# Vision tower, 64 images: the product of dt and x moves from GpSimd to VectorE, the order of work is laid out afresh, and the first loads are split

## What is computed

```python
h = patches(x) @ W.T + b                          # 16x16 patches of 3 colours
xb, z = split(h @ in_proj.T)                      # 512 channels each
xb = silu(causal_conv4(xb))
dt_in, B, C = split(xb @ x_proj.T)                # 1, 16 and 16 numbers a token
dt = softplus(dt_in * dt_w + dt_b)
h_n(t) = exp(dt * A_n) * h_n(t-1) + (xb * dt) * B_n    # 16 states a channel
y = sum_n h_n * C_n + xb * D
h = layernorm(h + (layernorm(y) * silu(z)) @ out_w.T)
h = layernorm(h + gated_ffn(h))                   # mixes each token with the one before it
h = layernorm(h + 8_head_attention(h))
h = layernorm(h + top2_of_8_experts(h))
```

## Time and profile before

| | us |
|---|---|
| median of 3 runs | 4496.96 (4495.98 to 4497.75) |
| span of the profiled execution, first to last instruction | 4498.6 |
| busy TensorE, GpSimd, ScalarE, VectorE | 4150.4, 4031.8, 3836.7, 3749.3 |
| mean granted TensorE clock over the span | 0.979 of full speed |

### The profile page before, as it was taken

The page is one execution under the profiler, slowest core; times in us unless marked ns, Lnnn a source line. Parts: engine busy times, 40 slices in busy tenths (PEclk is TensorE's granted clock), DMA queues, the critical chain, the costliest instruction groups (busy, mean ns, idle before and its releaser), DMA issues.

```text
span 4498.6 us, 92573 instructions
## 1 busy us (share of the span) xinstructions
PE 4150.4 (92%) x32128; PEld 3625.2 (81%) x32128; DVE 3749.3 (83%) x7246; ACT 3836.7 (85%) x10114; POOL 4031.8 (90%) x2120
## 2 busy tenths in 40 slices
PE   4689999999999999999999999999999999999986
PEld 3678888888888888888888888888888888888775
DVE  2678889888888888888988988888888888898853
ACT  3688988988988998898898898898899889889852
POOL 3999999999999999999999999999999999999930
PEclk8799999999999999999999999999999999999987
DMA  4332332233233233233233223323323323323200
GB/s 100 71 71 65 75 82 75 67 82 78 69 78 80 70 77 87 67 76 82 69 73 82 75 67 82 78 70 77 80 69 76 89 66 76 82 68 74 70 19 29
DMA packets 730609, 328.75 MB, mean 73 GB/s; under 512 B 631542, under 2 KB 655392, under 8 KB 729888
## 3 DMA queue, kind: packets, MB, share of 16 engines
q1 hardware_dynamic: 730144, 322.83, 29.1%
HBM read 307.82 MB, written 14.90 MB: 72 GB/s over the span
## 4 chain that ended last, share of the span: by engine, by line
PE 65%; ACT 19%; DVE 5%; POOL 5%; issue 3%; DMA 1%; SPq 1%; DVEq 0%; POOLq 0%; ACTq 0%
PE G L738 15%; PE YB L608 13%; PE G L575 6%; ACT dA L915 5%; PE SB L679 4%; PE G L660 4%; PE SB L584 4%; PE G L628 4%; PE G L652 3%; POOL X L497 2%; ACT pr L987 2%; PE SB L689 2%; POOL X L486 2%; DVE xbs L1110 2%; PE G L636 2%
## 5 line engine op out<-in xcount | busy, mean ns | idle before, releaser
L1145 DVE TENSOR_TENSOR_SCAN X<-dA,X 128x392 f32<-128x392 f32 x2048 | 1870.5, 955 | 142.0 <-ACT dA L915 96.7
L497 POOL TENSOR_TENSOR X<-X,Cb 128x1568 f32<-128x1568 f32 x512 | 1802.8, 3521 | 129.7 <-DVE X L1145 127.2
L486 POOL TENSOR_TENSOR X<-u,Bb 128x1568 f32<-128x1568 f32 x512 | 1804.2, 3524 | 0.1
L915 ACT ACTIVATE dA<-dt,negA 128x195 f32<-128x195 f32 x4096 | 1510.5, 414 | 64.6 <-DVE X L1145 46.0
L608 PE MATMUL YB<-idn,X 128*98 128x128 f32 x8192 | 1086.3, 276 | 23.6 <-POOL X L497 23.6
L608 PEld LDWEIGHTS YB<-idn,X 128*98 128x98 f32 x8192 | 908.2, 129 | 155.8 <-issue 102.1
L738 PE MATMUL G<-hg,we 128*128 128x196 f32 x4096 | 711.2, 332 | 8.3 <-DVE hg L1256 6.1
L738 PEld LDWEIGHTS G<-hg,we 128*128 128x128 f32 x4096 | 684.8, 192 | 10.8 <-issue 7.5
L987 ACT ACTIVATE pr<-pr,nmx 98x196 f32<-98x196 f32 x1024 | 453.4, 446 | 9.1 <-DVE nmx L1192 9.1
L584 PE MATMUL SB<-hT,win 128*128 128x196 f32 x2048 | 368.2, 333 | 14.5 <-ACT pT L998 5.6
L584 PEld LDWEIGHTS SB<-hT,win 128*128 128x128 f32 x2048 | 335.5, 190 | 29.5 <-issue 21.3
(11 more groups left out here) (151 smaller groups left out, 6554.7 us busy)
## 6 DMA issues: line engine op xcount, KB each, us to landing
Bb<-proj_rows SPq DMA_DIRECT2D x256, 392.0 KB, 4.2
Cb<-proj_rows SPq DMA_DIRECT2D x256, 392.0 KB, 3.8
Gb<-gate_rows SPq DMA_DIRECT2D x64, 784.0 KB, 4.1
px<-in_x SPq DMA_DIRECT2D x1024, 36.8 KB
out<-ob SPq DMA_DIRECT2D x64, 196.0 KB
dtin<-proj_rows SPq DMA_DIRECT2D x64, 98.0 KB, 3.0
we<-in_w_e SPq DMA_DIRECT2D x1, 2048.0 KB
proj_rows<-pj SPq DMA_DIRECT2D x64, 25.3 KB
```

The costliest lines, as they stand in the source:

```text
L486: tt(X[(WIDES * s + w) % RING][:], u[q % 2][:, c:c + 1, :].broadcast_to([P, NW, T]), Bb[:, n0:n0 + NW, :], ALU.mult).then_inc(xs_pool, 1)
L497: tt(t[:], t[:], Cb[:, n0:n0 + NW, :], ALU.mult).then_inc(prod_ready, 1)
L915: last = go(dA[i % DRING][:, j, 1:T], dt_[q % 2][:, c, 1:T], ACT.Exp, scale=negA[:, c, n:n + 1])
L1145: v.tensor_tensor_scan(t, dA[i % DRING].rearrange("p n t -> p (n t)"), t, 0.0, ALU.mult, ALU.add).then_inc(scan_done, 1)
```

## The change

1. `make_u` moves from GpSimd to VectorE. It reads dt and xbs, both in SBUF, and writes u. Its slot goes from -14 to -9, and GpSimd's wait for `xs_pool` in it falls away.
2. Nearly every slot constant and the order of the list in every `step` function are new. The work is the same, the six filling products of `keep_busy` among it.
3. The loads are split. ScalarE's queue issues six first (identity, patch weights, convolution and in_proj: `head`); SP issues the first image's pixels and then the other 26 loads. TensorE starts when the six have landed. VectorE scales the two convolution constants first (`conv_ready`), and prepares the other twelve inside `gate_x` of the first image; ScalarE waits for them in `tanh_of_x` of the first image (`late_weights`).

The diff, cut to its core:

```diff
-AT_LOAD = -46
-AT_PATCH = (-30, -28, -26,)
+AT_LOAD = -57
+AT_PATCH = (-30, -28, -27,)
...
-AT_EMBED = -25
+AT_EMBED = -24
...
-AT_U = -14
+AT_U = -9
...
-AT_ATT_STD = 59
-AT_ATT_NORM = 61
+AT_ATT_STD = 62
+AT_ATT_NORM = 66
...
-        loads = [(wtok, w_tok), (btok, b_tok), (win, w_in), (cw, conv_w), (cb, conv_b), (wxp, w_xproj),
+        head = [(idn, ident), (wtok, w_tok), (btok, b_tok), (cw, conv_w), (cb, conv_b), (win, w_in)]
+        loads = [(wxp, w_xproj),
...
-            def make_u(s, q):
-                pool.wait_ge(dt_ready, s + 1)
-                after(pool, xs_pool, WIDES * (s - 1))
-                tt(u[q % 2][:], dt_[q % 2][:], xbs[:], ALU.mult).then_inc(u_ready, 1)
...
+            def make_u(s, q):
+
+                dve.wait_ge(dt_ready, s + 1)
+                v.tensor_tensor(u[q % 2][:], dt_[q % 2][:], xbs[:], ALU.mult).then_inc(u_ready, 1)
...
-            pe.wait_ge(w_landed, W_ALL)
-            pe.wait_ge(const_ready, CONSTS)
+            pe.wait_ge(head_landed, W_HEAD)
...
+                if s == 0:
+                    late_weights()
                 go(S.tile, xbs[:].rearrange("p (a b) t -> p a (b t)", a=2), ACT.Tanh).then_inc(tanh_x, 1)
...
+            def late_weights():
+                act.wait_ge(w_landed, W_ALL)
+                go(negA[:], negA[:], ACT.Exp).then_inc(nega_exp, 1)
+                act.wait_ge(zeros_ready, ZEROS)
+                act.wait_ge(const_ready, CONSTS)
...
+            for dst, src in head:
+                act.dma_start(dst[:], src).then_inc(head_landed, 16)
+            act.wait_ge(head_landed, W_HEAD)
+            act.wait_ge(conv_ready, CONV)
```

More of the change, by code:

```diff
@@ L393, in _, with load_rest @@
         def _(sp):
+            def load_rest():
+                for dst, src in loads:
+                    sp.dma_start(dst[:], src).then_inc(w_landed, 16)
             def load(s):
@@ L437, in at @@
                         return live(b, par, g, slot)
+                    for s, q in at(AT_LOAD):
+                        load(s)
+                        if s == 0:
+                            load_rest()
                     for s, q in at(AT_DT_LOAD):
@@ L459, in step @@
                         spread_gates(s)
[L460 to L464, removed]
+                    for s, q in at(AT_PROJ_STORE):
+                        store_proj(s)
+                    for ng in range(GC):
+                        n0 = NG * ng
+                        for s, q in at(AT_C[ng]):
+                            after(sp, prod_ready, WIDES * s - WC + ng // 2 + 1)
+                            spread_rows(s, Cb[:, n0:n0 + NG, :], 1 + STATES + n0, NG, C_landed[ng])
             schedule(sp, step)
@@ L516, in step @@
                     for k in range(WIDES):
[L517 to L518 removed]
+                        for s, q in at(2 * k + AT_TIMES):
+                            times_c(s, k)
                     for s, q in at(AT_MOE_STD):
@@ L755, in at @@
                         return live(b, par, g, slot)
[L757 to L761, removed]
+                    for s, q in at(AT_V):
+                        pe.wait_ge(ksq_ready, s + 1)
+                        channel_major(s, "v", wv, ka)
+                    for s, q in at(AT_TURN_Y):
+                        turn_y(s)
+                    for s, q in at(AT_GATE):
+                        gate(s, q)
                     for s, q in at(AT_H1T):
@@ L764, in step @@
                         turn(s, "h1T", h1)
[L765 to L799, removed]
+                    for s, q in at(AT_EMBED):
+                        embed(s)
                     for s, q in at(AT_QK):
@@ L815, in step @@
                             scores(s, n)
[L816 to L820, removed]
+                    for s, q in at(AT_MOE_T):
+                        turn_moe(s)
+                    for part in range(3):
+                        for s, q in at(AT_PATCH[part]):
+                            patches(s, part)
+                    for s, q in at(AT_WARM[3]):
+                        keep_busy(WARM[3])
+                    for i in range(BLK):
+                        for s, q in at(AT_TURN_AV[i]):
+                            turn_values(s, i)
                     for s, q in at(AT_OUT):
@@ L1038, in step @@
                         drain_turned(s, "h3T", h3T[q % 2][:], where["h3T"].drained)
+                    for s, q in at(AT_ATT_NORM):
+                        if s > 0:
+                            filled("h3T2", s - 1)
+                        normalise(s, "att", lambda k: att[:, k, :], h3, normed["att"])
+                    for s, q in at(AT_Z_OUT):
+                        tanh_of_z(s)
+                    for part in range(3):
+                        for s, q in at(AT_PATCH_OUT[part]):
+                            drain_patches(s, part)
@@ new lines, in step @@
+                    for s, q in at(AT_KSQ):
+                        act.wait_ge(where["k"].drained, where["k"].count("k", s))
+                        go(ka[:], ka[:], ACT.Square).then_inc(ksq_ready, 1)
+                    for s, q in at(AT_YG):
+                        scale_y(s)
+                    for s, q in at(AT_EMBED_OUT):
+                        drain_embed(s, q)
+                    for s, q in at(AT_SOFT):
+                        softplus(s, q)
+                    for s, q in at(AT_TAP):
+                        first_tap(s)
@@ new lines, in step @@
+                    for s, q in at(AT_H2T_OUT):
+                        drain_turned(s, "h2T", h2T[:], where["h2T"].drained)
+                    for n in range(UNITS):
+                        for s, q in at(AT_PROBS[n]):
+                            probs(s, q, n)
+                    for s, q in at(AT_QK_OUT):
+                        drain_qk(s)
+                    for c in range(IC):
+                        for s, q in at(AT_Y_OUT[c]):
+                            drain_y(s, c)
+                    for s, q in at(AT_XPROJ_OUT):
+                        drain_proj(s)
@@ new lines, in step @@
+                    for s, q in at(AT_XD):
+                        times_d(s, q)
+                    for n in range(UNITS):
+                        for s, q in at(AT_PR[n]):
+                            drain_scores(s, n)
+                    for n in range(UNITS):
+                        for s, q in at(AT_PT[n]):
+                            drain_pT(s, n)
+                    for k in range(GROUPS):
+                        for s, q in at(k + AT_DECAY):
+                            decay(s, q, k)
@@ L1292, in step @@
                             taps(s, which)
+                    for s, q in at(AT_OUT_STATS):
+                        o = filled("outT", s)
+                        moments(s, "out", lambda k: o[0:TB, k * D:(k + 1) * D])
+                    for s, q in at(AT_MIX):
+                        token_mix(s)
+                    for s, q in at(AT_FFN_STATS):
+                        o = filled("ffnT", s)
+                        moments(s, "ffn", lambda k: o[0:TB, k * D:(k + 1) * D])
                     for i in range(BLK):
```

322 lines of the change are left out of this document (151 added, 171 removed).

## The result

The changed kernel takes **4631.27 us** (median; 4628.21 to 4632.74) against 4497.35 before: a ratio of 1.0295, 95% interval [1.028, 1.031]. It is 3% slower. Forecast were 4400 and a range of 4325 to 4500; the time lies outside, on the side of the third rival, which had put it at 4563.

What follows compares the result with a forecast made beforehand. It took a loop over ScalarE (some 15 us) and TensorE (51 us), 66.62 us an image, as the bound. 4498.6 - 82.6 (order) - 14 (start) = 4402.0, less 1.6 for the median: 4400 us; range 4325 to 4500.

Steps and rivals of the forecast that it cites:

- the third rival: u on VectorE and GpSimd's multiplications block each other, beyond 3.13 us it costs: slower, 4563 us; chance 0.14.
- u comes to VectorE: u on VectorE takes 0.97 us, hidden ahead of project_out and paid for before the scans; nothing added on the path.
- The far end: Upper bound for u on VectorE: it waits out a 3.52 us GpSimd multiplication, 4.49 us; GpSimd stands still 0.97.
- the low end: Lower bound for VectorE and GpSimd getting in each other's way over u: nothing, which the forecast took.
- Slots and orders: New slots and list orders on all engines: 1.4 us an image won, 82.6 us over 59 periods; bounds 0 and 156.
- the four covered waits: TensorE's waits at embed, turn_y, hT's transpose and the second patch transpose go, 1.77 us an image together.
- The floor of 63.97 us for TensorE: TensorE's period of 66.62 us less its 2.65 us of waits; with the same work it cannot go lower.
- the first rival: Another loop holds the period, new order opening as many waits as it shuts; only start won: 4483 us; chance 0.17.
- u leaves GpSimd: GpSimd's work falls from 63.0 to 61.15 us an image; alone worth nothing where TensorE holds the chain.
- The start: Split loads let TensorE start 16.5 to 21.2 us sooner; net gain taken as 14 us, bounds 0 and 18.
- A tanh at 30 to 33: Sign of a right forecast at the start: first tanh on ScalarE at 30 to 33 us, before at 48.87.

Runs made afterwards that it cites:

- e2: Changed kernel with u still on VectorE in the same place, but first operand from PSUM, dt left out for all but two images: 4459.48 us, ratio 0.9915.
- e4: Kernel before the change with only the start split (six loads on ScalarE's queue, the rest behind the first pixels): 4485.25 us, ratio 0.997.
- e1: Changed kernel with only u put back on GpSimd at slot -14; new order and split start stay: 4467.05 us, ratio 0.9928.
- e7: Changed kernel with u back on GpSimd and all of ScalarE's copies of y moved ahead of patches and softplus: 4588.35 us, ratio 1.0202.
- e9: Changed kernel with u back on GpSimd and only two of ScalarE's four copies of y moved ahead: 4455.95 us, ratio 0.9914.
- e10: Changed kernel with u on VectorE from PSUM (dt left out) and two copies of y moved ahead: 4453.66 us, median of three, ratio 0.99.
- e8: Changed kernel with u on VectorE from PSUM (dt left out) and all copies of y moved ahead: 4581.38 us, ratio 1.0184.
- e5: Changed kernel with u one place earlier in VectorE's order, between the two pairs of scans: 4499.71 us, ratio 1.0002.
- e6: Changed kernel with u two steps later in VectorE's order, behind the statistics and ahead of the last scans: 4579.77 us, ratio 1.0181.
- e3: Kernel before the change with only u moved to VectorE, ahead of gate_y, both inputs in SBUF; old order and start: 4652.04 us, ratio 1.0343.

## Why the prediction was wrong, point by point

**The step that failed** is in "u comes to VectorE": "I take nothing on the path, since u is one instruction an image." The far end stood beside it, 4.49 us for u and 0.97 for GpSimd. Measured are 3.49 and 0.72. One instruction an image is enough, because what stands behind it had too little slack: y, the scans, the taps and then ScalarE's qm and km follow in one chain. e2 against the changed kernel gives the price, with engine, place, size and count of u equal: periods of 66.32 and 69.05 us, so 59 x 2.73 = 161 of the 172 us. In the fill, where two u took 9.02 and 10.99 us, the chain falls 16 us behind (its first such product starts at 372.92 and not at 356.97). Together that is 5 us more than the 172, which this count does not settle. The choice of the low end went by zs, which has one operand in PSUM; the row was near in size and not in what mattered.

**The third rival** had the right mechanism and too low a price. It let 3.13 of 4.49 us be soaked up, by VectorE's 1.28 us of waiting and GpSimd's saved 1.85. At the measured 3.49 us its rule would have asked 0.36 us an image. Beside e2, next to nothing of u's lengthening was soaked up: u is 2.52 us longer, and the period 2.73. How much of this is GpSimd's 0.72 no run tells apart. GpSimd's saved 1.85 did not pay: its waits for scans grew by more than that, over 2 us an image (38.6 us against 17.6 in the window). So the rival's 4563 was 68 us too low.

The Trainium skill, page "SBUF — State Buffer", section "Who interferes with whom", was named for that rival: issue order decides who blocks, and the other side blocks fully. The traces agree in the steady part: u waits out the multiplication that it meets (3.49, 2.19 and 1.70 us in three places), and the next GpSimd instruction waits out u (4.25 for 3.53, 0.92 for 0.20). The same section says that a VectorE instruction with at most one SBUF input, outside certain modes, does not contend; the 967 ns of e2 agree.

**"Slots and orders", 1.4 us an image**, was mis-sized: e4 against e1 gives (66.61 - 66.33) = 0.28, with 66.61 = (4090.32 - 360.25) / 56 and 66.33 = (4080.86 - 366.14) / 56 from their chains. Each of the four covered waits did go. But adding up waits of TensorE is no sum of time: 1.92 us for ysb came in their place, and the wait for probs grew from 0.88 to 1.35. The nearest case is embed, whose 0.60 for patT the prediction took as covered by the D term and a group of sums. In e1 that D term (L615) itself waits, 0.63 of the 1.92 us, for a ysb that ScalarE copies right behind patT, so ScalarE's list still holds up embed (L585):

```profile
4054.45 0.10 ACT patT L866
...
4054.78 0.37 ACT ysb L942
...
4055.20 0.43 PE YB L615 x2
...
4056.50 3.98 PE G L585 x24
```

The floor of 63.97 us for TensorE did not hold either: in e1 it waits 1.92 + 1.35 = 3.27 of 66.33 us, which leaves 63.06; why the same products took less is not known. All this was the first rival, "a new order can open as many waits as it shuts", whose time of 4483 would have been near without the blocking (4459 to 4467). So even with u harmless the forecast was 60 us too low. e7 and e9 support it: with the waits on ysb taken away in part, others come, and in e9 the chain goes over VectorE's scans and taps, ScalarE's qm and km, TensorE, softplus and back. Which single handover closes that loop was not settled.

**"u leaves GpSimd": nothing** was right within the noise: e10 lies 2 us under e9, e8 7 under e7 and e2 8 under e1, each pair with overlapping intervals.

**"The start", 14 us** was near: 12.8 in e4. Partly that is luck, as its parts were off: the 16 pixel DMAs took 13.0 us to issue, more than the 6.7 to 11.4 assumed, so the first transpose came at 15.52 and not at 10 to 14, and the tanh at 36.63 and not at 30 to 33. TensorE started 15.3 us sooner, and the way from there to the tanh grew from 18.06 to 21.11. A tanh at 30 to 33 would have been 16 to 19 us sooner, so that sign did not fit the 14 either.

## What to carry to other kernels

Before an elementwise product moves to VectorE, look at where its operands lie: with both in SBUF and GpSimd multiplying nearly without a gap, it waited here for what was left of GpSimd's instruction (0.73 to 2.52 us in the steady part), and the next one of GpSimd, where it followed at once, became 0.72 us longer. If it must be there, put it where GpSimd is about to wait anyway (e5: 132 us for one place), or take one operand from PSUM (e2 shows the time of that, in a kernel that leaves dt out). And a list of waits on the fullest engine is not the gain of a new order: here 1.77 us of them went, and 0.28 came of it.

## What had not been expected of the hardware

VectorE is not always let in at the first boundary between two GpSimd instructions. In the fill of the changed kernel, u and GpSimd's multiplications:

```profile
210.53 10.99 DVE L1173 TENSOR_TENSOR u<-dt,xbs 128x784 f32<-128x784 f32 x1
```

```profile
210.27 3.50 POOL L491 TENSOR_TENSOR X<-u,Bb 128x1568 f32<-128x1568 f32 x1
213.73 3.49 POOL L502 TENSOR_TENSOR X<-X,Cb 128x1568 f32<-128x1568 f32 x1
217.18 3.51 POOL L491 TENSOR_TENSOR X<-u,Bb 128x1568 f32<-128x1568 f32 x1
225.58 0.19 POOL L507 TENSOR_TENSOR veps_ffn<-mv_ffn,epsc 98x2 f32<-98x2 f32 x1 [4.89 <-DVE mv_ffn L1191]
```

u stood through three multiplications, none of them stretched, and ended 0.83 us after the last (220.69), when GpSimd had nothing more to run. The third u took 9.02 us in the same way; in e5 and e6 four in the fill took 4.58 to 5.95, past one boundary. In e3, with the old order, no u took more than 3803 ns. From 260 us on all 60 of the changed kernel take 3473 to 3502 ns:

```profile
L1173 DVE TENSOR_TENSOR u<-dt,xbs x60: 3473/3494/3502, 284.1 to 4351.0; 128x784 f32<-128x784 f32 x60
```

What decides which of the two is let in at such a boundary stays open.
